# Routed experts of a decoder layer in blocks of 256 slots, with the weights as the stationary operand

## The reference, cut to what matters

```python
probs = softmax(flat @ gate_W.T)               # flat: x2 as [8192, 128], 8 experts
top_v, top_i = top_k(probs, 2)                 # two experts for each token
g = silu(einsum('td,edf->etf', flat, w1_e))    # per expert 128 -> 512
u = einsum('td,edf->etf', flat, w3_e)
out_e = einsum('etf,efd->etd', g * u, w2_e)    # 512 -> 128
routed = sum over the two experts of gate * out_e
shared = the same form with the shared weights w1_s, w3_s, w2_s, / 8
x = layernorm(x2 + 0.5 * shared + 0.5 * routed)
```

## Time and profile before

| | |
|---|---|
| median of 3 runs | 804.68 us (803.83 to 806.31) |
| the profiled execution's own time | 805.98 us |
| its span (first to last instruction) | 804.1 us |
| mean granted TensorE clock | 0.949 of 2.4 GHz |
| busy share: PE, DVE, ACT, POOL | 89%, 63%, 55%, 55% |
| first gather of `experts` / end of its last scatter | 317.13 / 711.70 us |

### The profile page before, as it was taken

One profiled execution on the slowest core, in us unless ns is written; L12 is line 12 of the kernel. 1 busy time (PEld: TensorE's weight loads), 2 busy tenths in 40 slices (PEclk: granted clock), 3 DMA queues, 4 the chain that ended last, 5 costly groups with the idle time before them and its releaser, 6 DMA issues. The chain is left out here.

```text
span 804.1 us, 18637 instructions
## 1 busy us (share of the span) xinstructions
PE 719.0 (89%) x4713; PEld 625.4 (78%) x4715; DVE 505.5 (63%) x2040; ACT 446.2 (55%) x1365; POOL 440.3 (55%) x461
## 2 busy tenths in 40 slices
PE   4789999966689997999999999999999999929990
PEld 3667888855578886888888888888888888828780
DVE  2798999983699996444444444444444444418996
ACT  4899999941322221455555555555555555516886
POOL 3378988872201111566666667766666676522322
PEclk9999999985799999999999999999999999968995
DMA  6467655732211130111111111111111111226653
GB/s 180 132 188 229 188 157 167 201 103 78 79 53 53 53 105 10 41 47 46 46 46 46 49 43 46 49 48 47 46 46 46 42 50 48 42 75 192 184 171 99
DMA packets 86849, 71.74 MB, mean 89 GB/s; under 512 B 9874, under 2 KB 72218, under 8 KB 86810
## 3 DMA queue, kind: packets, MB, share of 16 engines
q1 hardware_dynamic: 77808, 53.43, 22.3%
q0 software_dynamic: 8704, 17.84, 7.7%
q10 hardware_dynamic: 298, 0.01, 0.0%
HBM read 49.75 MB, written 21.50 MB: 89 GB/s over the span
## 5 line engine op out<-in xcount | busy, mean ns | idle before, releaser
L1196 POOL DMA_INDIRECT xg<-x_rows,src x136 | 131.7, 969 | 99.2 <-issue 61.3
L1341 DVE TENSOR_TENSOR e_h<-e_sg,bank 128x512 f32<-128x512 f32 x136 | 93.7, 689 | 133.8 <-PE bank L1239 106.6
L1202 POOL DMA_INDIRECT y_rows<-e_y,dst x136 | 134.2, 987 | 49.9 <-issue 38.0
L1303 ACT ACTIVATE e_sg<-bank 128x512 f32<-128x512 f32 x136 | 81.3, 598 | 136.7 <-PE bank L1239 136.6
L1279 PE MATMUL bank<-w,e_hT 128*128 x1088 | 143.9, 275 | 0.9 <-DVE e_y L1337 0.9
L1279 PEld LDWEIGHTS bank<-w,e_hT 128*128 128x128 f32 x1088 | 132.2, 192 | 1.3 <-issue 1.3
L1237 PE MATMUL bank<-w_hi,e_x_hi 128*128 x272 | 119.2, 438 | 0.0
L1239 PE MATMUL bank<-w_lo,e_x_hi 128*128 x272 | 108.7, 400 | 0.0
L1238 PE MATMUL bank<-w_hi,e_x_lo 128*128 x272 | 107.1, 394 | 0.0
L1308 ACT ACTIVATE e_hT<-bank 128x512 f32<-128x512 f32 x136 | 81.2, 597 | 23.0 <-PE bank L1270 23.0
L1270 PE MATMUL bank<-ident,e_h 128*128 128x128 f32 x544 | 81.5, 272 | 0.0
(11 more groups left out here) (168 smaller groups left out, 1646.8 us busy)
## 6 DMA issues: line engine op xcount, KB each, us to landing
yk<-y_rows SPq DMA_DIRECT2D x16, 512.0 KB, 4.3
xT_in<-in_xT_dram SPq DMA_DIRECT2D x16, 256.0 KB, 3.4
x_res<-in_x_dram SPq DMA_DIRECT2D x16, 256.0 KB, 3.7
w_in<-in_L_ffn_w_e_dram SPq DMA_DIRECT2D x16, 256.0 KB, 3.0
c_in<-in_ctx_dram SPq DMA_DIRECT2D x16, 256.0 KB, 2.9
cT_in<-in_ctxT_dram SPq DMA_DIRECT2D x16, 256.0 KB, 3.1
x_rows<-x SPq DMA_DIRECT2D x16, 256.0 KB, 2.4
x2T_cols<-x2T SPq DMA_DIRECT2D x16, 256.0 KB, 2.7
```

The source lines that it names most:

```text
L1196: nc.gpsimd.indirect_dma_start(xg[r][:, :], None, x2_rows, bass.IndirectOffsetOnAxis(src[r][:, 0:1], 0)).then_inc(gathered[r], 16)
L1202: nc.gpsimd.indirect_dma_start(y_rows, bass.IndirectOffsetOnAxis(dst[r][:, 0:1], 0), y[r][:, :], None).then_inc(scattered[r], 16)
L1303: nc.scalar.activation(sg[par][:, :], bank[par][:, :], ACT.Silu).then_inc(sg_ok, 1)
L1341: nc.vector.tensor_tensor(h[par][:, :], sg[par][:, :], bank[2 + par][:, :], ALU.mult).then_inc(h_ok, 1)
```

## The change

- `routing` pads each expert to blocks of BR = 256 slots: NB = 64 + 7 = 71 blocks, each of BT = 2 tiles of 128 rows. The row tables are NBT = 142 columns wide, `w_at` has 71 entries.
- In `experts` the weights become the stationary operand of the up products and the 256 tokens of a block the moving one. g and u then come out with the hidden units on the partitions, so h needs no transpose and no copy out of PSUM.
- PE's stationary operands have fixed addresses now: ACT copies the block's 1,024 columns of `w_hi` to one of two small tiles within SBUF, DVE does the same with `w_lo`. Each reads the block's place from `w_at` into a register of its own first.
- The copy of the result out of PSUM moves from DVE to ACT.
- POOL's program is written out in full, without a loop; its waits are constants, it reads `src_tab` and `dst_tab` in place, gathers eight blocks of 256 ahead, and issues two DMAs a block each way. The ring `xg` holds four blocks, and so does `y`.

```diff
-NB = T * K // P + E
+BT = 2
+BR = BT * P
+NB = T * K // BR + E - 1
+NBT = NB * BT
...
-        oh_blk = [sb(f"oh_blk{n}", [P, NB], BF16) for n in range(2 * OC)]
+        oh_blk = [sb(f"oh_blk{n}", [P, NBT], BF16) for n in range(2 * OC)]
...
 def experts(nc, sem, bank, m):
...
+        LOOP = (2, (NB - 3) // R)
...
+            for b in range(LOOP[0] * R):
                 step(b, b // R, b % R)
+            with engine.Fori(*LOOP) as j:
                 for r in range(R):
                     step(j * R + r, j, r, inner=True)
+            for b in range(LOOP[1] * R, NB + 2):
                 step(b, b // R, b % R)
...
         @block.gpsimd
+            def gather(b):
+                if b >= R:
+                    pool.wait_ge(xT_ps, b - R + 1)
+                for t in range(BT):
+                    n = b * BT + t
+                    nc.gpsimd.indirect_dma_start(xg[b % R][:, t, :], None, x2_rows,
+                                                 bass.IndirectOffsetOnAxis(src_tab[:, n:n + 1], 0)
+                                                 ).then_inc(gathered[b % R], 16)
+
+            def scatter(b):
+                pool.wait_ge(y_ok, b + 1)
+                for t in range(BT):
+                    n = b * BT + t
+                    nc.gpsimd.indirect_dma_start(y_rows, bass.IndirectOffsetOnAxis(dst_tab[:, n:n + 1], 0),
+                                                 y[b % R][:, t, :], None).then_inc(scattered[b % R], 16)
+
+            for b in range(2 * R):
+                gather(b)
+            for b in range(NB):
+                scatter(b)
+                if b + 2 * R < NB:
+                    gather(b + 2 * R)
...
         @block.tensor
             def transpose_x(b, j, r):
+                if not isinstance(b, int) or b >= 2:
+                    pe.wait_ge(x_lo_ok, b - 1)
+                pe.wait_ge(gathered[r], 16 * BT * (j + 1))
+                for t in range(BT):
+                    last = nc.tensor.transpose(bank[6 + r % 2][:, t * P:(t + 1) * P], xg[r][:, t, :], ident[:, :])
+                last.then_inc(xT_ps, 1)
+
+            def up(to, r, k, half):
+
+                for i in range(HC):
+                    w = slice(k * F + (half * HC + i) * P, k * F + (half * HC + i + 1) * P)
+                    at = to[:, i * BR:(i + 1) * BR]
+                    nc.tensor.matmul(at, w_hi[r % 2][:, w], x_hi[r][:, :], start=True, stop=False)
+                    nc.tensor.matmul(at, w_hi[r % 2][:, w], x_lo[r][:, :], start=False, stop=False)
+                    last = nc.tensor.matmul(at, w_lo[r % 2][:, w], x_hi[r][:, :], start=False, stop=True)
+                return last
...
+                    pe.wait_ge(w_hi_ok, b + 1)
+                    pe.wait_ge(w_lo_ok, b + 1)
                     pe.wait_ge(x_lo_ok, b + 1)
+                    for half in range(2):
+                        n = b * 2 + half
+                        if inner or b >= 1:
+                            pe.wait_ge(sg_ok, n - 1)
+                        up(bank[half], r, 0, half).then_inc(g_ps, 1)
+                        if inner or b >= 1:
+                            pe.wait_ge(h_ok, n - 1)
+                        up(bank[2 + half], r, 1, half).then_inc(u_ps, 1)
+                        if half == 0 and (inner or b + 2 < NB):
+                            transpose_x(b + 2, j + (r + 2) // R, (r + 2) % R)
+                    pe.reg_load(at_reg[par], w_at[0:1, ds(b, 1)])
                 if inner or 1 <= b <= NB:
+                    at = pe.snap(at_reg[other], min_val=0, max_val=(E - 1) * P)
+                    pe.wait_ge(h_ok, b * 2)
                     if inner or b >= 3:
                         pe.wait_ge(y_ok, b - 2)
+                    for t in range(BT):
+                        for c in range(FC):
+                            last = nc.tensor.matmul(bank[4 + other][:, t * D:(t + 1) * D],
+                                                    hT[other][:, c, t * P:(t + 1) * P],
+                                                    w2[:, :, :].rearrange("p e f -> p (e f)")[:, ds(at * (F // P) + c * D, D)],
+                                                    start=(c == 0), stop=(c == FC - 1))
                     last.then_inc(y_ps, 1)
...
         @block.scalar
+            def w_high(b, r):
+                act.reg_load(at_reg, w_at[0:1, ds(b, 1)])
+                at = act.snap(at_reg, min_val=0, max_val=(E - 1) * P)
+                if not isinstance(b, int) or b >= 2:
+                    act.wait_ge(u_ps, b * 2 - 2)
+                nc.scalar.activation(w_hi[r % 2][:, :], columns(w_hi_all, at), ACT.Copy).then_inc(w_hi_ok, 1)
...
+            def take_y(b, j, r):
+                act.wait_ge(y_ps, b + 1)
+                if not isinstance(b, int) or b >= R:
+                    act.wait_ge(scattered[r], 16 * BT * j)
+                nc.scalar.activation(y[r][:, :, :].rearrange("p t d -> p (t d)"), bank[4 + r % 2][:, 0:BT * D],
+                                     ACT.Copy).then_inc(y_ok, 1)
...
+                if inner or 2 <= b <= NB + 1:
+                    take_y(b - 2, j + (r - 2) // R, (r - 2) % R)
                 if inner or b < NB:
+                    silu(b * 2, 0, not inner and b < 1)
+                if inner or 1 <= b and b + 1 < NB:
+                    w_high(b + 1, (r + 1) % R)
+                if inner or b < NB:
+                    silu(b * 2 + 1, 1, not inner and b < 1)
                 if inner or b + 2 < NB:
+                    x_high(b + 2, (r + 2) % R)
...
         @block.vector
+            def w_low(b, r):
+                dve.reg_load(at_reg, w_at[0:1, ds(b, 1)])
+                at = dve.snap(at_reg, min_val=0, max_val=(E - 1) * P)
+                if not isinstance(b, int) or b >= 2:
+                    dve.wait_ge(u_ps, b * 2 - 2)
+                nc.vector.tensor_copy(w_lo[r % 2][:, :], columns(w_lo_all, at)).then_inc(w_lo_ok, 1)
...
                 if inner or b < NB:
+                    if inner or b >= 2:
+                        dve.wait_ge(y_ps, b - 1)
+                    hidden(b * 2, 0, par)
+                if inner or 1 <= b and b + 1 < NB:
+                    w_low(b + 1, (r + 1) % R)
+                if inner or b < NB:
+                    hidden(b * 2 + 1, 1, par)
                 if inner or b + 2 < NB:
+                    x_low(b + 2, (r + 2) % R)
```

More of the change, by code:

```diff
@@ L955, in table_of @@
                     at = c % 2 * OC + q
-                    last = nc.tensor.matmul(bank[6][:, 0:NB], oh_row[at][:, :], oh_blk[at][:, :],
+                    last = nc.tensor.matmul(bank[6][:, 0:NBT], oh_row[at][:, :], oh_blk[at][:, :],
                                             start=known == OG0 and c == 0 and q == 0, stop=True, skip_group_check=True)
@@ L1151, in experts @@
         R = 4
[L1152 to L1160, removed]
@@ L1162, in experts, with ring @@
-        src_ok = sem("e_src_ok")
+        HC = FC // 2
+        def ring(name, shape, dt=F32, n=R):
+            return [sb(f"e_{name}{i}", shape, dt) for i in range(n)]
+        xg = ring("xg", [P, BT, D])
+        y = ring("y", [P, BT, D])
+        x_hi = ring("x_hi", [P, BR], F32R)
+        x_lo = ring("x_lo", [P, BR], F32R)
+        w_hi = ring("w_hi", [P, 2 * F], F32R, n=2)
+        w_lo = ring("w_lo", [P, 2 * F], F32R, n=2)
+        sg = ring("sg", [P, HC * BR], n=2)
+        hT = ring("hT", [P, FC, BR], n=2)
@@ L1187, in steps, with columns @@
                 step(b, b // R, b % R)
+        def columns(w, at):
+            return w[:, :, :, :].rearrange("p e k f -> p (e k f)")[:, ds(at * (2 * F // P), 2 * F)]
         @block.gpsimd
         def _(pool):
[L1191 to L1211, removed]
-                    gather(b + 5, (r + 5) % R)
@@ L1225, in look_up @@
-            def look_up(b, par):
-                pe.reg_load(at_reg[par], w_at[0:1, ds(b, 1)])
-            def weights_at(regs, par):
-                return pe.snap(regs[par], min_val=0, max_val=(E - 1) * F)
-            def product(to, x, at):
-                def columns(w):
-                    return w[:, :, :, :].rearrange("p e k f -> p (e k f)")[:, ds(at, F)]
-                nc.tensor.matmul(to, x[0], columns(w_hi), start=True, stop=False)
-                nc.tensor.matmul(to, x[1], columns(w_hi), start=False, stop=False)
-                return nc.tensor.matmul(to, x[0], columns(w_lo), start=False, stop=True)
@@ new lines, in x_high, with silu @@
+            def x_high(b, r):
+                act.wait_ge(xT_ps, b + 1)
+                nc.scalar.activation(x_hi[r][:, :], bank[6 + r % 2][:, 0:BR], ACT.Copy).then_inc(x_hi_ok, 1)
+            def silu(n, half, first):
+                act.wait_ge(g_ps, n + 1)
+                if not first:
+                    act.wait_ge(h_ok, n - 1)
+                nc.scalar.activation(sg[half][:, :], bank[half][:, :], ACT.Silu).then_inc(sg_ok, 1)
+            def take_y(b, j, r):
[4 more added lines that the diff above has]
+                                     ACT.Copy).then_inc(y_ok, 1)
```

(8 more changed lines are left out.)

139 lines of the change are left out of this document (39 added, 100 removed).

## The result

| | before | after |
|---|---|---|
| median | 804.68 us (805.8 over the 8 runs beside it) | 794.33 us (8 runs, 792.87 to 799.2) |
| span of the profiled execution | 804.1 us | 792.7 us |
| first gather of `experts` / end of its last scatter | 317.13 / 711.70 us | 318.15 / 698.50 us |
| ratio after to before | | 0.9865, 95% interval 0.9843 to 0.9887 |

The change makes the kernel 1.4% faster, about 11 us. 781 was predicted, 24 us less than before: the direction and the range held, the gain was less than half of the forecast. Two of the eight executions of the kernel before took 1068 and 2542 us; they are left out of the ratio.

A forecast was written before the change was run, and what follows sets the result against it. PE bounds `experts` now, busy 388 of 395 us; POOL would bound it after. A gain of 37 us less 13 for the port leaves 24: 804.68 - 24 = 781 us, range 763 to 806 (8 of 10).

The forecast's parts named there:

- PE at 4.83 us a block: PE in `experts`: up products, transposes of x and down products sum to 4.83 us per 256 slots, against 5.68 now.
- Rival 3: PE in `experts`: weight loads don't hide behind 256 columns; 0.188 us a matmul, about 880 us; chance 0.06.
- ACT and DVE hidden: `experts`: ACT at 3.4 us and DVE at 2.8 us a block stay hidden under PE's 4.8 us.
- POOL becomes the pace: `experts`: POOL's 5.04 us a block exceeds PE's 4.83, so POOL bounds; PE idle 0.2 to 0.4 us a block.
- Rival 4: POOL in `experts`: gap shrinks between DMAs side by side; 1.0 us a DMA, PE bounds, 764 us; chance 0.08.
- POOL at 5.04 us a block: POOL in `experts`: two gathers at 1.25 us and two scatters at 1.27 us make 5.04 us a block.
- The port at 0.19 us a block: `experts`: DVE's `w_lo` copies hold POOL's DMAs 0.19 us a block, 12.7 us over 67 copies.
- The start: Start of `experts`: POOL begins at about 317.1 us as now; first result due about 335, wanted at 337.
- From the last gather to the end of the last scatter: End of `experts`: last gather near 655 us, last scatter ends about 675 us, before the port's cost.
- `combine` unchanged: Stage after `experts`: `combine` was forecast to take no change.
- Rival 1: POOL in `experts`: indirect DMAs don't need the port; 5.04 us a block, 768 us; chance 0.26.
- Rival 2: POOL in `experts`: port holds POOL for most of each copy; 795 us at 0.4 us, 814 at 0.69; chance 0.25.

The follow-up runs named there:

- experiment 4: Changed kernel with each block's second gather left out, PE transposing the first tile twice: 773.08 us, ratio to before 0.9599.
- experiment 1: Changed kernel with DVE's copies of `w_lo` left out from block 2 on (stale `w_lo` used): 779.79 us, ratio to before 0.9689.
- experiment 3: Changed kernel with the `w_lo` copy moved from DVE to ACT and the result copy from ACT to DVE: 779.03 us, ratio to before 0.9676.
- Experiment 7: Kernel before with only POOL's program written out, with constant waits: 806.86 us, ratio to before 1.0004.
- experiment 8: Version of experiment 3 with POOL's DMAs grouped, four scatters of two blocks, then four gathers: 779.67 us, ratio to before 0.9671.
- experiment 6: Kernel before plus a DVE copy of 128x1024 within SBUF into a spare tile every second block: 805.33 us, ratio to before 0.9989.
- experiment 5: Changed kernel without the `w_lo` copies from block 2 on, each DVE multiply of `hidden` done twice: 780.72 us, ratio to before 0.968.
- experiment 2: Changed kernel with a second DVE copy of the same size into a spare tile from block 2 on: 802.24 us, ratio to before 0.9959.

## Why the gain was 11 us and not 24

The steps of the prediction, in its order.

- **PE at 4.83 us a block**: 4.88 (experiment 4). The pitch of the up matmuls is 0.120 instead of 0.117, which over 24 is 0.07, and the down products are 1.71 instead of 1.62; the two transposes, 0.17 (504.05 to 504.22) instead of 0.22, give some of it back. Transposes that wait for nothing take 0.14 (385.95 to 386.09), and with these the sum is 4.88. That the load of the stationary operand hides behind 256 columns, argued from the down product's pitch, was right. Rival 3 is refuted.
- **ACT and DVE hidden**: right. PE waits for neither; the two copies have 1.06 and 0.69 us, as taken (1.09 and 0.69).
- **POOL becomes the pace**: right, and shown by experiments 1, 3 and 4. PE's idle time was forecast as 0.2 to 0.4 us in each block; it comes to 0.43 a block, but only from the 24th block on. Rival 4 is refuted: the gap of 0.30 us stands before DMAs side by side too.
- **POOL at 5.04 us a block: this step failed.** The prediction took 1.25 us for a gather from the first gathers, and explained their shorter record by their being written out. Experiment 7 shows that this has no effect, and experiment 8 that a DMA is longer behind one of the other kind. The mixed stream of the earlier trace rows had 0.97 and 0.99 with a gap of 0.30 each, which is 2 x (1.27 + 1.29) = 5.12 us. Measured without copies it is 5.147, so this term was 0.107 us too low, 63 x 0.107 = 6.7 us in sum.
- **The port at 0.19 us a block**: mechanism right, size nearly so. 0.222 is measured (experiment 1), 63 x 0.03 = 2.0 us more. The argument behind the 0.19 (a DMA caught by 0.55 of the copies and held for half of one) only resembles what happens: 37 of 70 copies stretch a DMA, by 0.1 to 0.5 us according to the moment at which they start (last section). That the two sizes are so near is in part luck.
- **The start**: the first scatter goes out at 339.26. The prediction has 337.35, and 0.76 for four of its 67 copies, the other 63 being in the pace; so it is 1.15 us late. The copies cost here what was counted: they stretch the first gather to 1.67 (from 1.20), the fifth to 1.22 and one at 332.89 to 1.07. What is left is POOL's own start, 1.0 us later than before; in the eleven traces of this study it lies anywhere from 315.88 to 318.15, so no effect of the change can be read from it.
- **From the last gather to the end of the last scatter**: 20.99 us (677.51 to 698.50), where the forecast went from 655 to 675, 1.0 us less. The terms that it lists for this part add up to 19.0 and would give 674.
- **`combine` unchanged**: from the last scatter's end to the end of the span are 94.2 us instead of 92.4, 1.8 more.

The sum: 1.15 + 6.7 + 2.0 + 1.0 + 1.8 = 12.7 us of the 24.1 that the last scatter was to come earlier (711.70 to 687.6) are lost. That leaves 11.4, as 804.1 - 792.7 = 11.4. The step that failed is thus the mis-sized base pace of POOL, which carries half of the miss; the port's own error is a sixth.

**The rivals.** Rival 1 (no port) is refuted by experiment 1. Rival 2 gave 795 us at 0.4 us a block, which is the time that came, but not for its reason: the price is 0.222 a block, and experiment 1 at 779.79 shows that the base was wrong instead. A prediction can meet a time by an error in one term that stands in for another.

**The rule of the Trainium skill** ("SBUF — State Buffer", section "SBUF: two separate sides": a float32 copy within SBUF on VectorE locks GpSimd out of their shared ports, so that it can't write the descriptors of its DMAs). The runs bear out its substance: the copy from SBUF to SBUF does it (experiments 1 and 6), work of DVE with an operand in PSUM doesn't (5), and a copy on ACT doesn't (3). They don't bear out a price of the copy's whole length. The same section says that whichever starts first keeps the port for its whole instruction; the DMA at 405.94 started first, and was stretched by a copy that began 0.47 us later and wasn't held.

**What stays open.** In all versions with blocks of 256 slots `combine` comes later behind the last scatter: 12.3 us to its first operation on POOL in the changed kernel, 12.7 and 12.6 in experiments 3 and 8, 15.0 in experiment 4, against 10.5 before and 10.9 with POOL written out (710.54 to 721.42). So it isn't the writing out. The difference lies ahead of the stage's first transfer, which SP issues 8.8 us behind the last scatter (707.28), against 6.75 before (718.45) and 10.9 in experiment 4 (685.33); what it is, no run here tells. Nor does a run tell whether the copy holds POOL because both its ends lie in SBUF or because of its rate (128x1024 in 0.69 us, as long as a multiply of 128x512): the work of experiment 5 differs from it in both. A gather of two rows for each partition in one DMA, which would take the fixed cost off POOL, was not tried.

## What to carry to other kernels

When a change moves the bound to another engine, take that engine's price for an instruction from the stream in which the instruction will stand, mixed as it will be, and not from a tidy stretch of one kind: 0.03 us a DMA was 0.1 us a block and 7 us of kernel. Before a float32 copy within SBUF goes to DVE, look whether POOL's queue has slack; where it has (experiment 6) the collision is free, and where POOL is the pace (experiment 3) the slower engine is the better place, 15 us here. Once two engines stand about 5% apart, as PE at 4.88 and POOL at 5.15 us a block, what is saved on one is soon capped by the other: experiment 4 takes a quarter of POOL's DMAs away and is 6 us below experiment 3. And an engine that works ahead hides the new bound for a while, so a block read early in a stage can show the wrong pace: over 20 blocks had gone through PE before POOL's pace reached it.

## What the runs showed of the hardware

- **The price of a copy depends on its phase.** Of the 70 copies from the second on in the trace of the changed kernel, by the start of the copy within the DMA that runs: 23 that start 0.26 to 0.53 us into a DMA stretch that one to 1.07 to 1.34 us, its offset plus 0.81, so that it ends 0.12 us behind the copy. 32 that start 0.56 to 0.82 us in don't stretch it, are for the most part held themselves, up to 0.91 us, and cost the next DMA 0.04 to 0.08. 14 that start 1.08 us in or later, in the gap, stretch the next DMA to 1.31 to 1.48. In experiment 2, copies that start 0.03 to 0.17 us in are free. The one of the 70 that is left starts 0.05 us in. The border just ahead of a DMA is sharp: eight copies of experiment 2 that start 0.01 to 0.03 us before one leave it at 0.96 and take 0.73 to 0.76 themselves, while those that start 0.04 or 0.05 us before one in experiment 6 stretch it to 1.47 to 1.50. The mean is about 0.21 us, from 0 to 0.5 for the same 0.69 us of copy. Which steps of a DMA need the port at those moments isn't told by these records.
- **Gathers and scatters in turn cost more than runs of one kind**: a gather is 0.99, 0.96, 0.94, 0.94 us by its place behind scatters, a scatter 1.00, 0.98, 0.97, 0.97 (experiment 8).
- **Weight loads with records of 0.192 us follow one another every 0.120 us** behind matmuls of 256 columns. The duration of such a record was no bound for the pace here.
